# A four-block graph network on one core: TensorE's products in up to three parts, and another order for four engines

## The chip, the core and the metric

One core of a Trainium2 chip runs the whole network in one program. The metric is the device time of that core in microseconds, from a launch; the profile is of one further execution. Five queues work in parallel and meet only by semaphores: TensorE (PE in the profile, its weight loads PEld), VectorE (DVE), ScalarE (ACT), GpSimd (POOL) and SyncE (SP), which issues the DMAs.

## What is computed

x is 128 graphs of 64 nodes with 384 features, adj a 0/1 matrix per graph. Four blocks follow each other, each on the normalized input and added to x:

```python
h = relu(layernorm(x)); x = x + L0(h, adj)        # two layers
h = relu(layernorm(x)); x = x + L1(h, adj, adj)   # 12 heads
h = relu(layernorm(x)); x = x + L2(h, adj)        # 12 heads
h = relu(layernorm(x)); x = x + L3(h, adj)        # two layers
# L0, a layer: u = h (h Wl)^T above and on the diagonal, h (h Wr)^T below, / sqrt(384)
#   e = exp(u) * adj;  ctx = (e / sum e) @ (h W + b);  h = relu(layernorm(ctx) * a + b)
# L1, L2: softmax(q k^T / sqrt(384) + bias) @ v, then @ Wo + bo
# L3, a layer: att = softmax(h h^T / sqrt(384)) * adj, each row divided by its sum
#   ctx = upper(att) @ (h Wl^T + bl) + diag(att) * (h Ws^T + bs) + lower(att) @ (h Wr^T + br)
#   h = relu(layernorm(ctx) * g + b)
```

All in float32. Each product with a weight matrix is made of three reduced-precision ones: weights and tokens are split into a high and a low part, and high x high, low x high and high x low are summed in PSUM.

## The kernel before

The 8192 tokens are 32 groups of 256 (four graphs). Two streams, 0 and 1, each with its own SBUF and PSUM (four banks), take the groups in turn, 16 rounds per phase. There are four phases, one for each block: GCN0 (`gcn0_phase`, line 411), twice attention (`attention_phase`, from 821) and GCN3 (`gcn3_phase`, from 1228). The activations go through DRAM between phases.

What an engine does for one stream and one round is cut into named stages. Each engine's order of stages is written out by hand, as a string for each of TensorE, ScalarE, VectorE and GpSimd (in this sequence in each list): `GCN0_ORDERS`, `ATT_ORDERS`, `GCN3_ORDERS` for a round, `BETWEEN` for the seam from one phase to the next. A word like `hT_1.1'` is stage hT of layer 1 for stream 1, and the mark ' says that it belongs to the round before. An engine runs its string strictly in order; a stage waits for semaphores at its start or inside, and the values that it waits for are counted from the strings (`Count`, `counts`). The first two rounds are written out, the other 14 are a loop; `w0` to `w5` in `BETWEEN` are the splits of the next phase's weight matrices.

Stages that the prediction speaks of:

- TensorE: `ml0..2`, `mr0..2`, `lin0..1` (GCN0), `q`, `k0..2`, `v`, `out` (attention), `w00..w21` (GCN3) are products: 9 matmuls for each of 256 columns (ml, mr, q, k: weights stationary) or 384 columns (lin, v, out, w: tokens stationary), issued by `exact_product` (L226). The nine are in three groups of three: the first six use the high part of the tokens, the last three the low part. `q` holds three such products, `v` and `out` two. `hT` are six transpositions (L726, L1096, L1616), `aT` one, `u` and `scores` the node by node products, `agg` and `pv` the sums over neighbours, `pt0..2` four transpositions each of the softmax (L1177; pv is L1191, scores L1160).
- VectorE: `split` cuts hT into its high and low part (L1496, L1498), `agg` makes the statistics of a layer norm (in GCN0 L689 and L694), `ln` applies them (L706 in GCN0, L1592 in GCN3, two instructions of 128x384 each), `out` adds the residual (L628, L1482: scalar_tensor_tensor of 128x768 with both tensors in SBUF), `v` takes v from PSUM (L1028), `beta` is L620.
- GpSimd: `agg` is one pow on 128x2 between VectorE's agg and ln (L514, L1366); `p` scales two thirds of the softmax (L924, before pt1 and pt2); `w0`, `w1` add a bias (L1347); `z` and `diag` are other elementwise steps.
- ScalarE: `hT`, `q`, `k`, `pt0..2` (L982), `pv` copy PSUM to SBUF; `norm` is the input's layer norm.

`hT_1` starts the second layer and waits for VectorE's `ln_0` of its stream:

```python
pe.wait_ge(dve_done[s], DV[s]("n_0", i))          # GCN0 and GCN3, hT of layer 1
pe.wait_ge(pool_done[s], PO[s](f"p{c}", i))       # attention, pt1 and pt2
pe.wait_ge(act_done[s], AC[s].all(i, ("pt0", 0), ("pt1", 0), ("pt2", 0)))   # pv
```

## Time and profile before

| | us |
|---|---|
| median of 3 runs (2810.28 to 2812.11) | 2811.89 |
| span of the profiled execution | 2807.3 |
| TensorE busy, matmuls (98% of the span) | 2738.0 |
| VectorE busy (72%) | 2029.9 |
| GpSimd busy (51%) | 1434.8 |
| ScalarE busy (46%) | 1281.6 |

TensorE issues 34304 matmuls and as many weight loads. A busy share is an average over the span: that TensorE is busy for 98% says that it is the bound and that 69 us of its span are idle, not where. Matmuls overlap in the profile, so an idle stretch between two is counted only from the modelled end of the first. The timelines give start and length of an instruction, or of a run of equal ones (x4), and in brackets the idle time before it and what released it.

### The profile page before, as it was taken

Reading aid. Unit: us, or ns where it says so; the run is one execution under the profiler, and the core shown is the slowest. Engines: PE = TensorE matmul, PEld = TensorE weight load, DVE = VectorE, ACT = ScalarE, POOL = GpSimd, SP = SyncE. Lnnn points to the kernel's source line nnn. Section 1 sums busy time; section 2 is a strip of 40 time slices with the busy share of each in tenths; the row PEclk is TensorE's granted clock in tenths of the full one; section 3 lists DMA queues with packets and bytes.
Section 4 is the critical chain, followed back from the end, with each engine's and each line's share of the span. In section 5 each row is a group of like instructions: output and inputs, shape, how many; then the busy total and the mean of one; then the engine's idle time right before and its main releaser. Section 6 shows DMA issues by size and latency. Waiting matters only on the chain.

```text
span 2807.3 us, 86091 instructions
## 1 busy us (share of the span) xinstructions
PE 2738.0 (98%) x34304; PEld 2536.4 (90%) x34304; DVE 2029.9 (72%) x3998; ACT 1281.6 (46%) x2069; POOL 1434.8 (51%) x2499
## 2 busy tenths in 40 slices
PE   7999999999999999999989999999999999999998
PEld 7999999999988999999989999999888888888887
DVE  4666666766687777777777777778667767776776
ACT  3334334334344444444444444444545545445443
POOL 1212212122224555555545555555777777778777
PEclk9999999999999999999999999999999999999999
DMA  4121121211112111111131111112112112111121
GB/s 155 43 78 45 56 67 41 82 41 62 62 55 84 49 49 49 49 49 49 43 101 49 49 49 49 49 49 68 39 39 75 37 42 70 37 64 48 37 75 34
DMA packets 116535, 158.88 MB, mean 57 GB/s; under 512 B 8048, under 2 KB 112368, under 8 KB 116464
## 3 DMA queue, kind: packets, MB, share of 16 engines
q1 hardware_dynamic: 116464, 157.88, 17.2%
q8 instruction: 51, 0.84, 0.1%
q14 instruction: 20, 0.16, 0.0%
HBM read 107.52 MB, written 50.33 MB: 56 GB/s over the span
## 4 chain that ended last, share of the span: by engine, by line
PE 52%; POOL 25%; issue 12%; DVE 5%; ACT 3%; DMA 1%; POOLq 1%; SPq 0%; DVEq 0%; ACTq 0%
PE ps L226 38%; POOL wide L1347 6%; POOL wide L933 5%; POOL wide L924 4%; PE ps L1160 3%; PE ps L786 2%; PE ps L1191 2%; POOL wide L1332 2%; PE ps L809 2%; POOL wide L1336 2%; PE ps L1177 2%; PE ps L726 2%; ACT wide L996 2%; POOL rstd L1366 1%; POOL x_rstd L891 1%
## 5 line engine op out<-in xcount | busy, mean ns | idle before, releaser
L226 PE MATMUL ps<-w_hi,split 128*128 128x384 f32 x4608 | 1269.2, 344 | 8.3 <-ACT wide L962 4.6
L226 PEld LDWEIGHTS ps<-w_hi,split 128*128 128x128 f32 x4608 | 847.5, 190 | 23.8 <-ACT wide L962 5.0
L226 PE MATMUL ps<-split,w_hi 128*128 128x256 f32 x4608 | 865.0, 283 | 1.7 <-DVE split L640 1.6
L226 PE MATMUL ps<-w_lo,split 128*128 128x384 f32 x2304 | 778.3, 338 | 1.6 <-issue 1.6
L226 PEld LDWEIGHTS ps<-split,w_hi 128*128 128x128 f32 x4608 | 724.5, 189 | 25.3 <-issue 13.8
L226 PE MATMUL ps<-split,w_lo 128*128 128x256 f32 x2304 | 575.5, 280 | 0.0
L226 PEld LDWEIGHTS ps<-w_lo,split 128*128 128x128 f32 x2304 | 436.5, 189 | 0.0
L226 PEld LDWEIGHTS ps<-split,w_lo 128*128 128x128 f32 x2304 | 435.4, 189 | 0.0
L933 POOL TENSOR_TENSOR wide<-wide 128x192 f32<-128x192 f32 x256 | 212.3, 858 | 405.3 <-ACT wide L996 405.3
L1347 POOL TENSOR_TENSOR wide<-wide,row 128x192 f32<-128x192 f32 x512 | 312.6, 645 | 29.8 <-ACT wide L1430 29.8
L514 POOL TENSOR_TENSOR rstd<-mv,pos_half 128x2 f32<-128x2 f32 x64 | 43.6, 691 | 453.4 <-DVE mv L694 453.4
L1430 ACT ACTIVATE wide<-ps 128x768 f32<-128x768 f32 x128 | 103.2, 806 | 248.3 <-PE ps L226 248.1
L924 POOL TENSOR_TENSOR wide<-wide,heads 128x512 f32<-128x512 f32 x128 | 163.4, 1296 | 82.0 <-DVE heads L1064 82.0
L996 ACT ACTIVATE wide<-ps 128x768 f32<-128x768 f32 x64 | 52.0, 812 | 239.7 <-PE ps L226 239.7
L982 ACT ACTIVATE wide<-ps 128x512 f32<-128x512 f32 x192 | 110.6, 598 | 102.2 <-PE ps L1177 54.7
L1077 DVE TENSOR_TENSOR split<-ps,split 128x384 fp32r<-128x384 f32 x128 | 65.4, 553 | 126.6 <-ACT split L991 126.5
L916 POOL TENSOR_TENSOR wide<-xin,bo_row 128x192 f32<-128x192 f32 x256 | 147.6, 609 | 3.6 <-DMA x_after<-wide 3.6
L972 ACT ACTIVATE wide<-wide 128x1536 f32<-128x1536 f32 x64 | 95.2, 1487 | 98.3 <-DVE wide L1047 98.3
L947 ACT ACTIVATE wide<-xin,x_shift,x_rstd 128x384 f32<-128x384 f32 x128 | 83.7, 701 | 100.9 <-POOL x_shift L894 100.9
L1177 PE MATMUL ps<-ident,wide 128*128 128x128 f32 x768 | 118.0, 278 | 8.2 <-POOL wide L924 5.9
L1496 DVE CAST split<-wide 128x768 fp32r<-128x768 f32 x64 | 42.4, 662 | 111.3 <-ACT wide L1394 66.3
L1036 DVE TENSOR_TENSOR wide<-ps,bias 128x1536 f32<-128x1536 f32 x64 | 112.0, 1749 | 11.2 <-PE ps L1160 11.1
(131 smaller groups left out, 4549.6 us busy)
## 6 DMA issues: line engine op xcount, KB each, us to landing
x_after<-wide SPq DMA_DIRECT2D x96, 384.0 KB, 2.5
xin<-x_after SPq DMA_DIRECT2D x96, 384.0 KB, 3.4
xin<-in_x SPq DMA_DIRECT2D x32, 384.0 KB, 4.1
wide<-in_x SPq DMA_DIRECT2D x32, 384.0 KB, 3.6
wide<-x_after SPq DMA_DIRECT2D x32, 384.0 KB, 4.1
out<-wide SPq DMA_DIRECT2D x32, 384.0 KB, 2.8
adjin<-in_adj SPq DMA_DIRECT2D x32, 256.0 KB, 3.6
w_raw<-in_w SPq DMA_DIRECT2D x3, 2304.0 KB, 13.7
```

The costliest lines, as they stand in the source:

```text
L226: last = nc.tensor.matmul(out, t if tokens_stay else w, w if tokens_stay else t, start=(k == 0), stop=(k == len(pairs) - 1))
L916: ins = nc.gpsimd.tensor_tensor(b.xout[:, rows, at], b.xin[:, rows, at], bo_row[:, at], ALU.add)
L924: nc.gpsimd.tensor_tensor(b.e_rows[:, c * n:(c + 1) * n], b.e_rows[:, c * n:(c + 1) * n], b.factor[:, c * n:(c + 1) * n].unsqueeze(2).broa ...
L933: ins = nc.gpsimd.tensor_tensor(b.xout[:, rows, at], b.xout[:, rows, at], b.o_raw[:, rows, at], ALU.add)
L972: nc.scalar.activation(b.e[:], b.e[:], ACT.Exp, scale=SCALE).then_inc(act_done[s], 1)
L982: nc.scalar.activation(b.pT[:, HPC * c:HPC * c + HPC], b.ps[:, c % 2, :], ACT.Copy)\
L996: nc.scalar.activation(b.o_raw, b.ps[:, 2:4, 0:FEAT], ACT.Copy).then_inc(act_done[s], 1)
L1036: nc.vector.tensor_tensor(b.s[:].rearrange("p c r k -> p r c k"), b.ps[:, :, 0:C * P].rearrange("p r (c k) -> p r c k", c=C), b.bias[:].re ...
L1160: mm = nc.tensor.matmul(b.ps[t * NODES:(t + 1) * NODES, r, c * P + gr * NODES:c * P + (gr + 1) * NODES], b.q[r * HD:(r + 1) * HD, c, at:at ...
L1177: mm = nc.tensor.transpose(b.ps[:, c % 2, r * P:(r + 1) * P], b.e[:, c, r], g.ident[:])
L1347: ins = nc.gpsimd.tensor_tensor(b.hw[:, rows, m, at], b.hw[:, rows, m, at], w_row[l][m][:, at], ALU.add)
L1430: nc.scalar.activation(b.hw[:, :, m], b.ps_w[m], ACT.Copy).then_inc(act_done[s], 1)
```

## The change

Every product can be issued in parts. `exact_product` gets a first and a last group out of three (a, b, c); `parted` and `pieces` make a stage for every run of groups, so that `lin0ab_1.0'` is the first six matmuls of `lin0` and `lin0c_1.0'` the last three. A part that begins a product waits as the product did, the part that ends it signals. No matmul is added or removed, and a stage without letters is the whole product. In attention `q`, `v` and `out` become `q0..q2`, `v0..v1` and `out0..out1`, in the same sequence.

The strings are another order of the same stages. In the rounds of GCN0, among others, TensorE's `hT_1.0'` and `hT_1.1'` come ahead of the last third of a product and agg_0.1' ahead of two thirds of ml2; VectorE's out.0' moves from behind lin_0.1 to between agg_0.1 and ln_0.1. In attention's rounds only TensorE's order changes: a third of k2 stands between pt1 and pt2. In GCN3 w20a_0.1 goes ahead of hT_1.0, hT_1.1 ahead of w20c_1.0, hT_0.1 ahead of most of w01 and w10, and the orders of ScalarE, VectorE and GpSimd change too. In the seams `v.0` stands ahead of `beta.1'` on VectorE (GCN0 to attention), v.0 is issued in four parts around pt0.1', pt1.1', pt2.1' and hT.1 (attention to attention), and scores.1' comes ahead of pt0.0', u_0.0 ahead of pt0.1' and ScalarE's w2 and w3 ahead of its pt stages (attention to GCN3).

The diff, without the second and third seam and without the like edits of the other product stages:

```diff
 GCN0_ORDERS = [
-    "ml0_0.1' mr0_0.1' agg_0.0' ml1_0.1' ml2_0.1' mr1_0.1' mr2_0.1' lin0_0.1' hT_1.0' u_0.1' lin1_0.1' "
-    "ml0_1.0' ml1_1.0' aT_0.1' ml2_1.0' agg_0.1' mr0_1.0' mr1_1.0' mr2_1.0' lin0_1.0' hT_1.1' u_1.0' "
-    "lin1_1.0' mr0_1.1' ml0_1.1' mr1_1.1' mr2_1.1' aT_1.0' ml1_1.1' ml2_1.1' hT_0.0 agg_1.0' u_1.1' "
-    "ml0_0.0 mr0_0.0 lin0_1.1' mr1_0.0 mr2_0.0 ml1_0.0 ml2_0.0 lin1_1.1' aT_1.1' u_0.0 agg_1.1' hT_0.1 "
-    "lin0_0.0 aT_0.0 lin1_0.0",
-    "hT_1.1' soft_1.0' norm.0 aT_1.0' mr_1.1' ml_1.1' hT_0.0 z_1.0' soft_1.1' mr_0.0 norm.1 ml_0.0 "
-    "aT_1.1' soft_0.0 hT_0.1 z_1.1' aT_0.0 z_0.0 ml_0.1 mr_0.1 hT_1.0 soft_0.1 aT_0.1 z_0.1 ml_1.0 mr_1.0",
-    "split_1.1' soft_1.0' stat.0 att_1.0' sum_1.0' lin_1.0' split_0.0 agg_1.0' soft_1.1' ln_1.0' att_1.1' "
-    "stat.1 lin_1.1' sum_1.1' soft_0.0 att_0.0 gain.0' beta.0' split_0.1 lin_0.0 sum_0.0 agg_1.1' agg_0.0 "
-    "ln_0.0 split_1.0 soft_0.1 att_0.1 lin_0.1 out.0' sum_0.1 ln_1.1' agg_0.1 ln_0.1 gain.1' beta.1' "
-    "out.1'",
-    "agg_0.1' stat.0 agg_1.0' stat.1 adj_1.1 adj_0.0 adj_0.1 agg_0.0 agg_1.1' adj_1.0",
+    "ml0_0.1' mr0_0.1' ml1a_0.1' agg_0.0' ml1bc_0.1' ml2_0.1' mr1_0.1' mr2_0.1' lin0ab_0.1' hT_1.0' "
+    "lin0c_0.1' u_0.1' lin1_0.1' ml0_1.0' ml1ab_1.0' aT_0.1' ml1c_1.0' ml2a_1.0' agg_0.1' ml2bc_1.0' "
+    "mr0_1.0' mr1_1.0' mr2_1.0' lin0ab_1.0' hT_1.1' lin0c_1.0' u_1.0' lin1ab_1.0' mr0a_1.1' "
+    "lin1c_1.0' mr0bc_1.1' ml0_1.1' mr1_1.1' mr2_1.1' ml1ab_1.1' aT_1.0' ml1c_1.1' ml2_1.1' hT_0.0 "
+    "agg_1.0' u_1.1' lin0a_1.1' ml0_0.0 mr0_0.0 mr1_0.0 mr2_0.0 lin0b_1.1' ml1_0.0 ml2ab_0.0 "
+    "lin0c_1.1' ml2c_0.0 lin1_1.1' aT_1.1' u_0.0 agg_1.1' hT_0.1 lin0_0.0 aT_0.0 lin1_0.0",
+    "hT_1.1' soft_1.0' norm.0 aT_1.0' mr_1.1' ml_1.1' hT_0.0 z_1.0' soft_1.1' mr_0.0 ml_0.0 norm.1 "
+    "aT_1.1' soft_0.0 hT_0.1 z_1.1' aT_0.0 z_0.0 ml_0.1 mr_0.1 hT_1.0 soft_0.1 aT_0.1 z_0.1 ml_1.0 "
+    "mr_1.0",
+    "split_1.1' soft_1.0' stat.0 att_1.0' sum_1.0' lin_1.0' split_0.0 soft_1.1' agg_1.0' ln_1.0' "
+    "att_1.1' stat.1 lin_1.1' soft_0.0 sum_1.1' att_0.0 gain.0' split_0.1 beta.0' lin_0.0 sum_0.0 "
+    "agg_1.1' agg_0.0 ln_0.0 split_1.0 soft_0.1 att_0.1 lin_0.1 sum_0.1 ln_1.1' agg_0.1 out.0' "
+    "ln_0.1 gain.1' beta.1' out.1'",
+    "agg_0.1' stat.0 agg_1.0' stat.1 adj_1.1 adj_0.0 adj_0.1 agg_1.1' agg_0.0 adj_1.0",
 ]
 ATT_ORDERS = [
-    "q.1' k0.1' k1.1' v.1' pt0.0' hT.0 pt1.0' pt2.0' k2.1' pv.0' scores.1' out.0' q.0 k0.0 k1.0 v.0 "
-    "pt0.1' hT.1 pt1.1' pt2.1' k2.0 pv.1' scores.0 out.1'",
-    "q.1' norm.0 pt0.0' hT.0 pt1.0' pt2.0' k.1' pv.0' out.0' exp.1' q.0 norm.1 pt0.1' hT.1 pt1.1' pt2.1' "
-    "k.0 pv.1' out.1' exp.0",
-    "stat.0 abs.0' fac.0' v.1' hT.0 pv.0' s.1' soft.1' stat.1 abs.1' fac.1' v.0 hT.1 pv.1' s.0 soft.0",
+    "q0.1' q1.1' q2.1' k0.1' k1.1' v0.1' v1.1' pt0.0' hT.0 pt1.0' k2a.1' pt2.0' k2bc.1' pv.0' "
+    "scores.1' out0.0' out1.0' q0.0 q1.0 q2.0 k0.0 k1.0 v0.0 v1.0 pt0.1' hT.1 pt1.1' k2a.0 pt2.1' "
+    "k2bc.0 pv.1' scores.0 out0.1' out1.1'",
+    "q.1' norm.0 pt0.0' hT.0 pt1.0' pt2.0' k.1' pv.0' out.0' exp.1' q.0 norm.1 pt0.1' hT.1 pt1.1' "
+    "pt2.1' k.0 pv.1' out.1' exp.0",
+    "stat.0 abs.0' fac.0' v.1' hT.0 pv.0' s.1' soft.1' stat.1 abs.1' fac.1' v.0 hT.1 pv.1' s.0 "
+    "soft.0",
     "bias.1' stat.0 bias.0 p.0' xb.1' out.0' stat.1 p.1' xb.0 out.1'",
 ]
 GCN3_ORDERS = [
-    "hT_0.0 agg_1.0' u_0.0 aT_1.1' w20_1.1' w21_1.1' w00_0.0 w01_0.0 w10_0.0 hT_0.1 w11_0.0 u_0.1 "
-    "agg_1.1' aT_0.0 w20_0.0 w21_0.0 w00_0.1 agg_0.0 aT_0.1 w01_0.1 w10_0.1 w11_0.1 hT_1.0 w20_0.1 "
-    "w21_0.1 w00_1.0 w01_1.0 agg_0.1 u_1.0 w10_1.0 w11_1.0 w20_1.0 hT_1.1 w21_1.0 u_1.1 aT_1.0 w00_1.1 "
-    "w01_1.1 w10_1.1 w11_1.1",
-    "soft_0.1' swap_0.1' on_0.0' tiny_0.1' w0_0.1' w1_0.1' hT_1.0' on_0.1' w0_1.0' swap_1.0' w1_1.0' "
+    "hT_0.0 agg_1.0' u_0.0 aT_1.1' w20_1.1' w21_1.1' w00_0.0 w01a_0.0 hT_0.1 w01bc_0.0 w10_0.0 "
+    "w11_0.0 u_0.1 agg_1.1' aT_0.0 w20_0.0 w21_0.0 w00_0.1 agg_0.0 aT_0.1 w01_0.1 w10_0.1 w11_0.1 "
+    "w20a_0.1 hT_1.0 w20bc_0.1 w21_0.1 w00_1.0 w01_1.0 agg_0.1 u_1.0 w10_1.0 w11_1.0 w20ab_1.0 "
+    "hT_1.1 w20c_1.0 w21_1.0 u_1.1 aT_1.0 w00_1.1 w01_1.1 w10_1.1 w11_1.1",
+    "soft_0.1' on_0.0' swap_0.1' tiny_0.1' w0_0.1' w1_0.1' hT_1.0' on_0.1' w0_1.0' swap_1.0' w1_1.0' "
     "tiny_1.0' soft_1.0' hT_1.1' soft_1.1' tiny_1.1' swap_1.1' w0_1.1' norm.0 hT_0.0 on_1.0' w1_1.1' "
     "soft_0.0 swap_0.0 norm.1 w0_0.0 hT_0.1 on_1.1' w1_0.0 tiny_0.0",
-    "sum_1.0' diag_1.0' split_1.1' soft_1.1' stat.0 w2_1.0' att_1.1' sum_1.1' stat.1 aT_1.0' split_0.0 "
-    "diag_1.1' aT_1.1' soft_0.0 agg_1.0' w2_1.1' att_0.0 ln_1.0' split_0.1 soft_0.1 sum_0.0 diag_0.0 "
-    "aT_0.0 agg_1.1' w2_0.0 att_0.1 sum_0.1 agg_0.0 diag_0.1 ln_0.0 split_1.0 aT_0.1 w2_0.1 ln_1.1' "
-    "agg_0.1 out.0' ln_0.1 soft_1.0 out.1' att_1.0",
-    "agg_0.1' on_1.0' diag_1.0' adj_0.0 w0_1.0' stat.0 on_1.1' w1_1.0' stat.1 adj_1.0 w0_1.1' w1_1.1' "
-    "adj_0.1 diag_1.1' agg_1.0' adj_1.1 w0_0.0 on_0.0 w1_0.0 diag_0.0 z.0' on_0.1 agg_1.1' agg_0.0 "
-    "diag_0.1 w0_0.1 w1_0.1 z.1'",
+    "sum_1.0' diag_1.0' split_1.1' soft_1.1' stat.0 att_1.1' sum_1.1' stat.1 w2_1.0' aT_1.0' "
+    "diag_1.1' split_0.0 soft_0.0 agg_1.0' aT_1.1' att_0.0 w2_1.1' split_0.1 ln_1.0' soft_0.1 "
+    "sum_0.0 diag_0.0 agg_1.1' att_0.1 aT_0.0 w2_0.0 sum_0.1 agg_0.0 ln_0.0 diag_0.1 aT_0.1 "
+    "split_1.0 w2_0.1 ln_1.1' agg_0.1 out.0' ln_0.1 soft_1.0 out.1' att_1.0",
+    "agg_0.1' on_1.0' diag_1.0' adj_0.0 w0_1.0' stat.0 w1_1.0' on_1.1' adj_1.0 stat.1 w0_1.1' "
+    "w1_1.1' agg_1.0' adj_0.1 diag_1.1' adj_1.1 w0_0.0 on_0.0 w1_0.0 diag_0.0 on_0.1 z.0' agg_0.0 "
+    "agg_1.1' diag_0.1 w0_0.1 w1_0.1 z.1'",
 ]
 BETWEEN = [
     [
-        "ml0_0.1' agg_0.0' mr0_0.1' ml1_0.1' ml2_0.1' mr1_0.1' mr2_0.1' hT_1.0' lin0_0.1' u_0.1' lin1_0.1' "
-        "aT_0.1' ml0_1.0' agg_0.1' ml1_1.0' ml2_1.0' mr0_1.0' mr1_1.0' mr2_1.0' hT_1.1' lin0_1.0' u_1.0' "
-        "mr0_1.1' ml0_1.1' lin1_1.0' aT_1.0' mr1_1.1' mr2_1.1' ml1_1.1' ml2_1.1' agg_1.0' u_1.1' lin0_1.1' "
-        "lin1_1.1' aT_1.1' hT.0 agg_1.1' q.0 hT.1 k0.0 k1.0 v.0 k2.0 scores.0",
-        "hT_1.1' w0 w1 w2 soft_1.0' aT_1.0' norm.0 mr_1.1' ml_1.1' z_1.0' soft_1.1' aT_1.1' hT.0 z_1.1' "
-        "norm.1 w3 hT.1 q.0 k.0 exp.0",
-        "split_1.1' soft_1.0' stat.0 att_1.0' w0 sum_1.0' lin_1.0' stat.1 w1 w2 agg_1.0' soft_1.1' att_1.1' "
-        "ln_1.0' lin_1.1' sum_1.1' hT.0 gain.0' beta.0' out.0' agg_1.1' hT.1 ln_1.1' gain.1' w3 beta.1' v.0 "
-        "out.1' s.0 soft.0",
+        "ml0_0.1' mr0a_0.1' agg_0.0' mr0bc_0.1' ml1_0.1' ml2_0.1' mr1_0.1' mr2_0.1' hT_1.0' "
+        "lin0_0.1' u_0.1' lin1_0.1' ml0ab_1.0' aT_0.1' ml0c_1.0' ml1a_1.0' agg_0.1' ml1bc_1.0' "
+        "ml2_1.0' mr0_1.0' mr1_1.0' mr2_1.0' lin0a_1.0' hT_1.1' lin0bc_1.0' u_1.0' lin1a_1.0' "
+        "mr0_1.1' ml0_1.1' mr1a_1.1' lin1bc_1.0' mr1bc_1.1' aT_1.0' mr2_1.1' ml1_1.1' ml2_1.1' "
+        "agg_1.0' u_1.1' hT.0 lin0_1.1' lin1_1.1' q0a.0 aT_1.1' q0b.0 agg_1.1' q0c.0 q1.0 q2.0 "
+        "k0ab.0 hT.1 k0c.0 k1.0 v0.0 v1.0 k2.0 scores.0",
+        "hT_1.1' soft_1.0' w0 w1 w2 aT_1.0' norm.0 mr_1.1' ml_1.1' z_1.0' hT.0 soft_1.1' aT_1.1' w3 "
+        "z_1.1' norm.1 q.0 hT.1 k.0 exp.0",
+        "split_1.1' soft_1.0' stat.0 att_1.0' sum_1.0' stat.1 lin_1.0' w0 w1 w2 agg_1.0' soft_1.1' "
+        "ln_1.0' att_1.1' lin_1.1' hT.0 sum_1.1' gain.0' w3 beta.0' agg_1.1' hT.1 ln_1.1' out.0' "
+        "gain.1' v.0 beta.1' out.1' s.0 soft.0",
         "agg_0.1' stat.0 stat.1 bias.0 agg_1.0' agg_1.1' xb.0",
     ],
...
@@ -214,18 +223,42 @@
     return not isinstance(i, int) or i > 0
 
 
-def exact_product(nc, out, terms, tokens_stay=False, tokens_lo_made=None):
+PARTS = "abc"
+
+
+def parted(stages):
+
+    return {piece: (whole, first, last) for whole in stages for first in range(len(PARTS))
+            for last in range(first, len(PARTS))
+            for piece in {whole + PARTS[first:last + 1]} | ({whole} if last - first == len(PARTS) - 1 else set())}
+
+
+def ends(events):
+
+    return {piece: names for whole, names in events.items() for piece, (_, _, last) in parted([whole]).items()
+            if last == len(PARTS) - 1}
+
+
+def pieces(stages):
+
+    def cut(stage, first, last):
+        return lambda s, i: stage(s, i, first, last)
+    return {piece: cut(stages[whole], first, last) for piece, (whole, first, last) in parted(stages).items()}
+
+
+def exact_product(nc, out, terms, first, last, tokens_stay=False, tokens_lo_made=None):
 
 
 
     pairs = [(w, t_hi) for w_hi, w_lo, t_hi, _ in terms for w in (w_hi, w_lo)]
     pairs += [(w_hi, t_lo) for w_hi, _, _, t_lo in terms]
-    for k, (w, t) in enumerate(pairs):
+    for k in range(len(terms) * first, len(terms) * (last + 1)):
+        w, t = pairs[k]
         if k == 2 * len(terms) and tokens_lo_made is not None:
             tokens_lo_made()
-        last = nc.tensor.matmul(out, t if tokens_stay else w, w if tokens_stay else t,
-                                start=(k == 0), stop=(k == len(pairs) - 1))
-    return last
+        mm = nc.tensor.matmul(out, t if tokens_stay else w, w if tokens_stay else t,
+                              start=(k == 0), stop=(k == len(pairs) - 1))
+    return mm
 
 
 class Shared:
...
             def ml(o):
-                def stage(s, i):
-                    if o == 0:
+                def stage(s, i, first, last):
+                    if o == 0 and first == 0:
                         weights_made(pe, g, phase, 3 * l + LEFT, i)
                         pe.wait_ge(dve_done[s], DV[s](f"t_hi_{l}", i))
-                    mm = project_T(s, i, bufs[s].rows[l], LEFT, o)
-                    if o == C - 1:
+                    mm = project_T(s, i, bufs[s].rows[l], LEFT, o, first, last)
+                    if o == C - 1 and last == len(PARTS) - 1:
                         mm.then_inc(pe_done[s], 1)
                 return stage
 
...
-        def q(s, i):
-            def tokens_lo_made():
-                pe.wait_ge(dve_done[s], DV[s]("t_lo", i))
-            pe.wait_ge(act_done[s], AC[s]("t_hi", i))
-            o_taken(s, i, 0)
-            weights_made(pe, g, phase, WQ, i)
-            project_T(bufs[s], bufs[s].ps_row, WQ, chunks=(0, 1), tokens_lo_made=tokens_lo_made)
-            o_taken(s, i, 1)
-            project_T(bufs[s], bufs[s].ps_row, WQ, chunks=(2,)).then_inc(pe_done[s], 1)
-
-        def k(c):
-            def stage(s, i):
-                if c == 0:
+        def q(o):
+            def stage(s, i, first, last):
+                def tokens_lo_made():
+                    pe.wait_ge(dve_done[s], DV[s]("t_lo", i))
+                if first == 0:
+                    if o == 0:
+                        pe.wait_ge(act_done[s], AC[s]("t_hi", i))
+                        o_taken(s, i, 0)
+                        weights_made(pe, g, phase, WQ, i)
+                    if o == C - 1:
+                        o_taken(s, i, 1)
+                mm = project_T(bufs[s], bufs[s].ps_row, WQ, o, first, last, tokens_lo_made=tokens_lo_made)
+                if o == C - 1 and last == len(PARTS) - 1:
+                    mm.then_inc(pe_done[s], 1)
+            return stage
+
...
```

## Rows read from the trace of the kernel before

**Rows 1.** stretches: length, then busy us of PE, PEld, DVE, ACT, POOL, clock, DMA

```profile
40.00:790.00 750.00, 749.68 (x8174) 687.98 (x8172) 497.89 (x1317) 293.45 (x545) 159.29 (x360) 1.00 0.18 60
790.00:912.00 122.00, 111.61 (x1664) 105.72 (x1663) 99.96 (x153) 54.24 (x82) 48.95 (x72) 0.97 0.26 80
912.00:1370.00 458.00, 454.41 (x7835) 438.73 (x7835) 359.94 (x448) 220.92 (x316) 259.75 (x395) 1.00 0.15 48
1975.00:2760.00 785.00, 778.48 (x6166) 689.41 (x6166) 554.00 (x1393) 393.85 (x673) 598.63 (x1088) 1.00 0.15 50
```

**Rows 2.** who TensorE waited for: idle us in total, times, longest

```profile
PE ps L1616 <- DVE wide L1592: 7.0, 15, 0.5
PE ps L1177 <- POOL wide L924: 5.9, 26, 0.2
PE ps L226 <- ACT wide L962: 4.6, 2, 2.3
PE ps L1160 <- DVE wide L1028: 2.1, 1, 2.1
```

**Rows 3.** timeline of a GCN0 round: start us, us, engine, line; TensorE, VectorE, GpSimd

```profile
450.79 0.69 PE L226 MATMUL ps<-w_hi,split 128*128 128x384 f32 x3
451.32 0.82 PE L726 MATMUL ps<-ident,wide 128*128 128x128 f32 x6
...
448.90 0.15 DVE L694 BATCH_NORM_AGGREGATE mv<-st 128x2 f32<-128x6 f32 x1
450.26 0.87 DVE L706 TENSOR_SCALAR wide<-wide,mv,rstd 128x384 f32<-128x384 f32 x2
...
449.13 0.69 POOL L514 TENSOR_TENSOR rstd<-mv,pos_half 128x2 f32<-128x2 f32 x1 [10.62 <-DVE mv L694]
```

**Rows 4.** timeline of a GCN3 round about hT_1.0; VectorE, GpSimd, TensorE

```profile
2351.40 1.56 DVE L1592 TENSOR_SCALAR wide<-wide,mv,rstd 128x384 f32<-128x384 f32 x2 [0.62 <-POOL rstd L1366]
...
2351.48 2.49 POOL L1347 TENSOR_TENSOR wide<-wide,row 128x192 f32<-128x192 f32 x4
...
2353.02 0.87 PE L1616 MATMUL ps<-ident,wide 128*128 128x128 f32 x6 [0.48 <-DVE wide L1592]
```

**Rows 5.** the same round about hT_1.1; VectorE, GpSimd, TensorE

```profile
2364.49 0.96 DVE L1482 SCALAR_TENSOR_TENSOR wide<-wide 128x768 f32<-128x768 f32 x1
...
2366.04 0.87 DVE L1592 TENSOR_SCALAR wide<-wide,mv,rstd 128x384 f32<-128x384 f32 x2 [0.60 <-POOL rstd L1366]
...
2364.54 1.47 POOL L1366 TENSOR_TENSOR rstd<-rstd,neg_half 128x2 f32<-128x2 f32 x1 [0.52 <-DVE rstd L1567]
...
2367.19 0.82 PE L1616 MATMUL ps<-ident,wide 128*128 128x128 f32 x6
```

**Rows 6.** timeline of attention about pt2 and pv, rounds and seam; TensorE, ScalarE

```profile
1200.72 0.65 PE L1177 MATMUL ps<-ident,wide 128*128 128x128 f32 x4 [0.23 <-POOL wide L924]
1201.13 0.36 PE L226 MATMUL ps<-split,w_hi 128*128 128x256 f32 x1
...
1202.36 0.45 PE L1191 MATMUL ps<-wide 64*32 64x64 f32 x31
...
1200.80 1.21 ACT L982 ACTIVATE wide<-ps 128x512 f32<-128x512 f32 x2
...
1219.77 0.34 PE L1191 MATMUL ps<-wide 64*32 64x64 f32 x16
...
1218.37 1.08 ACT L982 ACTIVATE wide<-ps 128x512 f32<-128x512 f32 x2
...
1396.79 0.60 ACT L982 ACTIVATE wide<-ps 128x512 f32<-128x512 f32 x1 [0.32 <-PE ps L1177]
...
1397.53 0.69 PE L1191 MATMUL ps<-wide 64*32 64x64 f32 x48
```

**Rows 7.** timeline of VectorE ahead of v.0 in the first seam

```profile
827.52 1.20 DVE L620 TENSOR_TENSOR wide<-wide,row 128x768 f32<-128x768 f32 x1
828.65 0.94 DVE L1028 TENSOR_TENSOR wide<-ps,bv_row 128x768 f32<-128x768 f32 x1
```

172 lines of the change are left out of this document (97 added, 75 removed), and 31 rows, old and new, of the table BETWEEN.

## The prediction

> **What bounds the kernel now.** I read the windows by phase first: what each engine does there, and how much of the stretch TensorE is idle [rows 1]. In the rounds of the first phase TensorE is idle for 0.3 us of 750; in the first attention phase's rounds for 3.6 of 458; in the last phase's for 6.5 of 785; the seam into attention loses 10 of 122, with the granted clock at 0.97. VectorE is busy for two thirds to four fifths, so only TensorE is a bound by its work. What a reordering can win is therefore what TensorE waits for. The list of its waits says for whom [rows 2]: hT_1 of the last phase for the layer norm on VectorE (L1592, 15 times), pt2 of attention for GpSimd's scaling (L924, 26 times), and the seams. The rest comes from short timelines of one steady round per phase. The idle column starts at the modelled end of the last matmul, and a transposition that waits for nothing starts 0.16 us before that end: the row of three products at 450.79 ends at 451.48, hT_1.1 starts at 451.32 [rows 3]. So a wait of 0.48 in the list costs 0.64. The same two rows give the length of a third of a product with 384 columns: 0.53 us.
>
> **Last phase, hT_1.0.** Its input is ready at 2352.96 (L1592 starts at 2351.40 and takes 1.56) and it starts at 2353.02, 0.06 later, with 0.48 of idle before it [rows 4]. The change puts w20a_0.1 in front: 0.53 of 0.64 are covered. The two L1592 take 0.87 together elsewhere [rows 5], and 1.56 here because GpSimd's L1347 runs beside them from 2351.48 [rows 4]. The new GpSimd order puts the small agg_1.1' (a pow on 128x2, 0.69 in [rows 3]) ahead of diag_0.1 and w0_0.1, so that L1347 begins some 0.7 later and the norm should be ready earlier than TensorE gets there: I take the whole wait as gone, 15 x 0.64 = -9.6. Bounds: -15 x 0.53 if the norm stays at 1.56, and the loss of the third rival. What is late next is the split behind hT_1.0, because w00_1.0 follows 0.53 sooner: 0 to 0.2 a round, I take 0.07, +1.0.
>
> **Last phase, hT_1.1.** It moves ahead of w20c_1.0, 0.53 earlier. Its input (L1592 from 2366.04 for 0.87) is ready at 2366.91, and it started at 2367.19 [rows 5]. It would now be issued at 2366.66 and wait until 2366.97: 0.31. Queued behind it are w20c, w21 and u_1.1; the last then has 0.5 more cover for its own input, so I take 0.25: 15 x 0.25 = +3.8. Why its input is late stands in the same rows: out.0' (L1482, both inputs in SBUF, 0.96) starts at 2364.49 on VectorE, the pow L1366 starts 0.05 later on GpSimd and takes 1.47 in place of 0.69.
>
> **First phase, hT_1.1.** Before, VectorE ran out.0' ahead of sum_0.1, and agg_0.1 was followed by ln_0.1 at once: statistics end at 449.05, the pow takes 0.69 from 449.13, ln_0.1's large pair (L706) ends at 451.13, hT_1.1 starts at 451.32 [rows 3]. The new VectorE order is agg_0.1 out.0' ln_0.1, the pair that costs 1.47 in the last phase, with the same form of instruction (L628 as L1482, 128x768 from SBUF) and the same start order. The new TensorE order issues agg_0.1 six 256-column products earlier (six of the nine in 1.23 us [rows 6], 0.7 to 0.8; I take 0.70), so the statistics end at 448.35 and the pow starts 0.08 later, at 448.43, as before. With 1.47 [rows 5] it ends at 449.90; L706 starts 0.44 after a pow's end and takes 0.87 [rows 3]: 451.21, and 0.06 to TensorE: 451.27. TensorE gets there at 451.32 - 0.53 = 450.79. Wait 0.48, of which I take 0.47; nothing else of TensorE may pass it, and its rounds had no slack. Without out.0' behind it (round 0) and in the seam, where more products stand between, it doesn't appear: 14 x 0.47 = +6.6. Bounds 0 (pow at 0.69) and +6.6. The other thirds in this phase fill no wait, since there was none; I cost them at 0, hidden by the products that follow.
>
> The Trainium skill (SBUF — State Buffer, Who interferes with whom) says that a VectorE instruction with two SBUF inputs contends with a GpSimd instruction that reads SBUF. The 1.47 against 0.69 agrees, and it speaks against this change. The same section says that the loser blocks for the whole instruction; the 1.56 of L1592 beside three L1347 is less than that would give, and the rows decide.
>
> **Attention.** In round 10, stream 0, pt2 waits for GpSimd until 1200.72: 0.23 of idle, 0.39 with the overlap. k2a (a third of the nine products between 1201.13 and 1202.36, 0.41) now stands before it and covers that. But pv is next, 0.41 sooner, and it needs ScalarE's two L982 that end at 1202.01 [rows 6]. How soon pv follows such a copy shows in the seam: copy ended at 1397.39, pv at 1397.53, 0.14 [rows 6]. So pv starts at 1202.01 + 0.03 + 0.14 = 1202.18 where it started at 1202.36: 0.18 of 0.39 is won, and the rest becomes a wait for ScalarE. In stream 1 the copies end at 1219.45 and pv starts at 1219.77; the products now push pt2 and its copy back by 0.15, and nothing is won. Net 0.17 a round, 28 rounds of the two phases: -4.7. Bounds: 0, and -28 x 0.6 if the copies weren't in the way. q, v and out in single parts have the same instructions: 0. ScalarE's, VectorE's and GpSimd's orders of these rounds don't change.
>
> **Seams and start.** Into attention scores.0 waits 2.1 for v.0 on VectorE [rows 2]. v.0 (from 828.65) stood behind beta.1' (1.20, [rows 7]) and moves ahead of it, but s.0, which heads the chain to the next 2.3 us wait, then stands behind beta.1' and out.1': of 1.2 I keep 1.0. Between the attention phases the parts of v.0 now stand ahead of pt1.1 and pv.1, which waited for copies there (0.32 of idle before the one, 0.12 before the other, each with its 0.16 of overlap [rows 6]): -0.6, the rest of it in the bounds. Into the last phase u_0.0 loses pt0.1' as its cover, four transpositions, 0.41 as those from 1200.72 to 1201.13 [rows 6]: +0.4; w2 and w3 on ScalarE ahead of the pt copies are hidden behind out.0', which waits for VectorE's pv.0' (L1077) in any case; at the start ml1a covers 0.3 of agg_0.0's wait. Together -1.5, bounds -5 and +2. The waits with no releaser and the stretches at the lower clock stay.
>
> **The sum.** -9.6 + 1.0 + 3.8 + 6.6 - 4.7 - 1.5 = -4.4 us. The profiled span is 2807.3, the median of the runs 2811.9: I apply the difference to the median, 2807.5, -0.16%.
>
> **Rivals.** (1) out.0' and the pow don't meet as in the last phase (the pow takes 0.69): no wait at hT_1.1 in either phase, -4.4 - 6.6 - 3.8 = -14.8, 2797.1. For it: in the first phase the order before never had the two together. Against: same form, same order, and the 1.47 is in the rows. 0.20. (2) The thirds only move waits: attention gives 0 (pv takes all of it), the seams 0: 2813.7. For it: 0.35 and 0.32 between copy and pv is all the room there is. 0.20. (3) Slower: the pow of agg_1.1', now just ahead of ln_0.0, holds VectorE instead of L1347 doing so. The norm then ends 0.69 later, at 2353.65, hT_1.0 waits 2353.71 - 2352.91 = 0.80 instead of 0.64, and -9.6 becomes +2.4: +7.6, 2819.5. It decides from a wait of 0.70 at hT_1.0. By the rule of the section named above this is what should happen if the pow issues first. Against: pow and norm read little of what the other holds, and the norm beside nothing but a pow isn't in the rows. 0.15. My own case 0.40; 0.05 for what I don't see.
>
> **Numbers.** About 0.2% (5.6 us) is what a measurement of this kernel can tell from no change. My case spans 2802 to 2812 and lies on both sides of that bound: nearly half of it counts as faster. Faster 0.18 + 0.20 = 0.38, within 0.2% 0.44, slower 0.18. The range takes in rival 1 and most of the way to rival 3: 2797 to 2818.
>
> **What would show it.** In the list of waits: L1616 for L1592 down in total but some 0.15 each at hT_1.1; a new line L726 for L706, 14 times 0.3; L1177 for L924 nearly gone; L1191 for L982 up to about 30 entries. GpSimd's L514 at 1.47 fourteen times. I am wrong if L514 stays at 0.69 throughout, if L1592 is at or above 0.7 at ln_0.0, or if the rounds of any phase hold a wait on an operation not named here, such as w2_1.1' ahead of hT_0.1, which moves 15 products forward.

## The result, and the profile after

The changed kernel takes 2825.5 us (median of 4 runs, 2823.6 to 2828.0) where the kernel before, timed beside it, takes 2811.1 (2809.5 to 2812.1): a ratio of 1.0051, 95% interval 1.0038 to 1.0064. The forecast was 2807.5 with a range of 2797 to 2818. The time is 14.4 us above the kernel before and outside the range, and even the rival that ended slower, 2819.5, fell short of it.

The span of the profiled execution is 2824.4 us. The totals hardly differ from before, and the list of what TensorE waited for is the first thing to read (columns: idle us in total, times, longest; rows of the start and the seams left out at the dots):

```profile
PE 2746.0 (97%) x34304; PEld 2535.7 (90%) x34304; DVE 2032.7 (72%) x3998; ACT 1283.9 (45%) x2069; POOL 1461.1 (52%) x2499
...
PE ps L1660 <- DVE small L1586: 7.4, 14, 1.8
...
PE ps L760 <- DVE wide L740: 5.6, 25, 0.2
...
PE ps L1743 <- DVE wide L1551: 3.4, 14, 1.1
...
PE ps L1219 <- POOL wide L959: 0.9, 2, 0.7
```

Lines have moved by 33 to 48: L760 is hT of the first phase, L740 its `ln`; L1660 is hT of the last phase, L1586 the copy of aT, L1551 `w2`, L1743 `agg`; L1219 is pt, L959 GpSimd's scaling. The two large rows of [rows 2] are gone as forecast (L1592, 15 times; L924 from 26 times to 2). In their place stand three rows that the forecast has only in part: hT_0.0 for aT's copy, hT_1 of the first phase 25 times and not 14, and `agg` for `w2`.

The windows say in which phase it happens (stretches as in [rows 1]):

```profile
40.00:790.00 750.00, 744.22 (x8038) 673.39 (x8037) 494.49 (x1295) 288.22 (x536) 162.82 (x355) 1.00 0.18 59
790.00:912.00 122.00, 114.26 (x1556) 107.94 (x1556) 98.70 (x168) 54.37 (x81) 47.00 (x73) 0.97 0.24 76
912.00:1370.00 458.00, 454.79 (x8026) 442.60 (x8024) 362.07 (x447) 222.82 (x319) 258.93 (x395) 1.00 0.15 49
1975.00:2760.00 785.00, 772.95 (x6150) 679.27 (x6150) 543.99 (x1365) 390.36 (x666) 608.57 (x1068) 1.00 0.15 50
```

TensorE's idle time grew from 0.3 to 5.8 us in the first phase's stretch and from 6.5 to 12.1 in the last's. The clock is the same, stretch by stretch.

The sharpest measure is the length of a round: from the start of stream 0's input transposition (hT_0.0, in attention hT.0) in round 4 to that in round 14, a tenth of it. It agrees within 0.15 us between kernels with the same orders, and 14 times the sum of the differences (attention twice, for its two phases) gives each total below within 3.5 us, e12 (5) and e7 (10) apart. For the change: 14 x (0.98 + 0.79) - 28 x 0.38 = 14.1, of 14.4 measured.

| kernel | median us | ratio to before, 95% | GCN0 | attention | GCN3 |
|---|---|---|---|---|---|
| before | 2811.1 | | 49.63 | 34.96 | 51.48 |
| changed | 2825.5 | 1.0038 to 1.0064 | 50.61 | 34.58 | 52.27 |
| e1_stat1_behind | 2812.6 | 1.0001 to 1.0019 | 50.58 | 34.59 | 51.40 |
| e2_pow_first | 2818.1 | 1.0021 to 1.0050 | 50.04 | 34.60 | 52.33 |
| e3_out_back | 2817.5 | 1.0018 to 1.0038 | 50.16 | 34.59 | 52.40 |
| e4_tensor_rounds | 2798.0 | 0.9955 to 0.9979 | 49.80 | 34.59 | 51.37 |
| e5_others_rounds | 2830.9 | 1.0067 to 1.0097 | 50.39 | 34.95 | 52.57 |
| e6_seams_only | 2806.9 | 0.9980 to 0.9998 | 49.70 | 34.95 | 51.49 |
| e7_fixes | 2827.0 | 1.0042 to 1.0072 | 49.66 | 34.59 | 52.76 |
| e8_diag_behind | 2798.4 | 0.9941 to 0.9967 | 49.70 | 34.95 | 50.83 |
| e9_best | 2793.5 | 0.9918 to 0.9945 | 49.70 | 34.60 | 50.95 |
| e10_three_back | 2799.8 | 0.9947 to 0.9974 | 49.80 | 34.59 | 51.39 |
| e11_two_thirds | 2809.9 | 0.9991 to 1.0009 | 49.67 | 35.19 | 50.83 |
| e12_out1_early | 2830.3 | 1.0050 to 1.0077 | 50.64 | 34.59 | 52.37 |
| e13_diag_and_thirds | 2798.3 | 0.9940 to 0.9974 | 49.69 | 34.60 | 51.41 |
| e14_best_seams | 2788.2 | 0.9912 to 0.9947 | 49.67 | 34.59 | 50.84 |

The kernel before, run beside them, had medians of 2808.8 (e1 to e8), 2809.6 (e9 to e12) and 2810.2 us (e13, e14).

**Where the last phase lost it.** One steady round about hT_0.0 (VectorE, then SyncE's DMAs, then TensorE):

```profile
2378.24 0.95 DVE L1526 SCALAR_TENSOR_TENSOR wide<-wide 128x768 f32<-128x768 f32 x1
...
2386.23 1.02 DVE L1511 BATCH_NORM_STATS2 x_st<-xin 128x6 f32<-128x384 f32 x2 [1.08 <-DMA xin<-x_after]
...
2387.45 0.92 DVE L1551 TENSOR_TENSOR wide<-ps,row 128x768 f32<-128x768 f32 x1
2388.30 0.41 DVE L1586 TENSOR_TENSOR small<-ps,parts 128x256 f32<-128x256 f32 x1
...
2379.38 0.40 SPq L367 DMA_DIRECT2D out<-wide  x1
...
2381.43 0.37 SPq L356 DMA_DIRECT2D xin<-x_after  x1
...
2388.76 0.87 PE L1660 MATMUL ps<-ident,wide 128*128 128x128 f32 x6 [0.59 <-DVE small L1586]
```

out.1' (L1526) ends at 2379.19. Only then can SyncE store it (2379.38), and the load of x for the next round is issued behind the store (2381.43). stat.1 (L1511) reads that x and starts 7.04 us after out.1' has ended, having stood idle for 1.08. The change put w2_1.0' (L1551, 0.92) behind stat.1 and ahead of aT_1.0' (L1586), for which hT_0.0 waits. The kernel before had the same load, with stat.1 (L1467 there) 6.9 us behind out.1', but w2_1.0' (L1507) ran while it was under way, VectorE stood for 0.1 only, and aT_1.0' (L1542) followed stat.1 at once:

```profile
2373.22 0.93 DVE L1507 TENSOR_TENSOR wide<-ps,row 128x768 f32<-128x768 f32 x1
...
2375.18 1.02 DVE L1467 BATCH_NORM_STATS2 x_st<-xin 128x6 f32<-128x384 f32 x2
...
2376.40 0.39 DVE L1542 TENSOR_TENSOR small<-ps,parts 128x256 f32<-128x256 f32 x1
```

The 0.92 has moved from beside the load to behind it.

**Where the first phase lost it.** One round about both hT_1 (VectorE, GpSimd, TensorE):

```profile
441.75 0.41 DVE L734 TENSOR_SCALAR rstd<-rstd 128x2 f32<-128x2 f32 x1 [0.80 <-POOL rstd L548]
...
442.40 1.18 DVE L740 TENSOR_SCALAR wide<-wide,mv,rstd 128x384 f32<-128x384 f32 x2
...
453.82 0.96 DVE L662 SCALAR_TENSOR_TENSOR wide<-wide 128x768 f32<-128x768 f32 x1
...
455.77 0.87 DVE L740 TENSOR_SCALAR wide<-wide,mv,rstd 128x384 f32<-128x384 f32 x2
...
441.68 0.46 POOL L534 TENSOR_TENSOR small<-adjin,ones 128x128 f32<-128x128 f32 x1
442.10 0.88 POOL L539 TENSOR_TENSOR small<-adjin,tri 128x128 f32<-128x128 f32 x2
453.95 1.38 POOL L548 TENSOR_TENSOR rstd<-mv,pos_half 128x2 f32<-128x2 f32 x1 [10.96 <-DVE mv L728]
...
443.64 0.87 PE L760 MATMUL ps<-ident,wide 128*128 128x128 f32 x6 [0.23 <-DVE wide L740]
...
456.69 0.88 PE L760 MATMUL ps<-ident,wide 128*128 128x128 f32 x6 [0.22 <-DVE wide L740]
```

The second half is the forecast: the pow beside out.0' (L662) takes 1.38, and hT_1.1 waits. The first half isn't in it: adj_1.0 (L534, L539) now follows the pow of agg_0.0 at once and runs beside ln_0.0. It costs twice there. The small L734 at the head of ln_0.0, which starts 0.07 behind L534, takes 0.41 where it takes 0.17 in ln_0.1 and in the kernel before, and the two L740 take 1.18 where they took 1.02 before (0.87 in ln_0.1). Together that is 0.4, and hT_1.0 waits as well.

### The profile page after: what moved, and what is told of

The parts are those of the page before. It is cut to its first block, busy times and chain, and to the rows that moved or that the text cites. A ratio compares the mean times of both kernels' runs of the same rounds, so it can differ in the third digit from the quotient of the medians.

```text
span 2824.4 us, 86091 instructions
## 1 busy us (share of the span) xinstructions
PE 2746.0 (97%) x34304; PEld 2535.7 (90%) x34304; DVE 2032.7 (72%) x3998; ACT 1283.9 (45%) x2069; POOL 1461.1 (52%) x2499
## 4 chain that ended last, share of the span: by engine, by line
PE 65%; issue 12%; POOL 11%; DVE 7%; DMA 3%; ACT 1%; SPq 1%; POOLq 0%; DVEq 0%; ACTq 0%
PE ps L259 48%; POOL wide L1391 4%; PE ps L1219 3%; PE ps L1202 3%; PE ps L1233 3%; PE ps L820 2%; PE ps L843 1%; PE ps L1743 1%; DMA xin<-x_after 1%; PE ps L1131 1%; PE ps L760 1%; POOL wide L1376 1%; POOL wide L1380 1%; POOL rstd L1410 1%; DMA adjin<-in_adj 1%
## 5 line engine op out<-in xcount | busy, mean ns | idle before, releaser
L259 PE MATMUL ps<-split,w_lo 128*128 128x256 f32 x2304 | 589.8, 284 | 0.0
L1391 POOL TENSOR_TENSOR wide<-wide,row 128x192 f32<-128x192 f32 x512 | 343.2, 705 | 39.4 <-ACT wide L1474 39.4
L548 POOL TENSOR_TENSOR rstd<-mv,pos_half 128x2 f32<-128x2 f32 x64 | 54.5, 851 | 460.4 <-DVE mv L728 460.4
L959 POOL TENSOR_TENSOR wide<-wide,heads 128x512 f32<-128x512 f32 x128 | 165.0, 1308 | 81.7 <-DVE heads L1099 81.7
L982 ACT ACTIVATE wide<-xin,x_shift,x_rstd 128x384 f32<-128x384 f32 x128 | 83.7, 701 | 98.6 <-POOL x_shift L929 98.5
L1071 DVE TENSOR_TENSOR wide<-ps,bias 128x1536 f32<-128x1536 f32 x64 | 112.0, 1749 | 12.3 <-PE ps L1202 12.1
L1219 PE MATMUL ps<-ident,wide 128*128 128x128 f32 x768 | 117.8, 276 | 1.4 <-POOL wide L959 0.9
```

The lines of the kernel that those rows point to most:

```text
L259: mm = nc.tensor.matmul(out, t if tokens_stay else w, w if tokens_stay else t, start=(k == 0), stop=(k == len(pairs) - 1))
L959: nc.gpsimd.tensor_tensor(b.e_rows[:, c * n:(c + 1) * n], b.e_rows[:, c * n:(c + 1) * n], b.factor[:, c * n:(c + 1) * n].unsqueeze(2).broa ...
L1071: nc.vector.tensor_tensor(b.s[:].rearrange("p c r k -> p r c k"), b.ps[:, :, 0:C * P].rearrange("p r (c k) -> p r c k", c=C), b.bias[:].re ...
L1219: mm = nc.tensor.transpose(b.ps[:, c % 2, r * P:(r + 1) * P], b.e[:, c, r], g.ident[:])
L1391: ins = nc.gpsimd.tensor_tensor(b.hw[:, rows, m, at], b.hw[:, rows, m, at], w_row[l][m][:, at], ALU.add)
```

## The experiments

The theory after the result: the new orders of VectorE and GpSimd lose what TensorE's new order gains, at three single stages. The rival: TensorE's own order makes the waits, by taking transpositions out from behind the products that covered their inputs.

**e1_stat1_behind.** The changed kernel, last phase, VectorE:

```diff
-... sum_1.1' stat.1 w2_1.0' aT_1.0' diag_1.1' ...
+... sum_1.1' w2_1.0' aT_1.0' stat.1 diag_1.1' ...
```

> The changed kernel with one stage moved in the last phase's VectorE order: stat.1 behind aT_1.0' instead of ahead of w2_1.0'. Theory: the 0.59 us a round that hT_0.0 waits there for aT_1.0' (7.4 us in 14 waits in the list) is VectorE standing before stat.1, 1.08 us in the round shown, for a load of x that lands later, with w2_1.0' and aT_1.0' queued behind it. Then hT_0.0's wait is gone: 14 x 0.59 = 8.3 less, 2825.5 - 8.3 = 2817, 1.002 of the kernel before. Rival: aT_1.0' is late because VectorE as a whole is late at this place (it is busy from out.1' on), and stat.1 merely takes its turn elsewhere: then hT_0.0 keeps 0.5 or more a round, or the same wait turns up at a later stage, and the time stays within 2 us of 2825.5.

2812.6 us, and 0.87 off the round. VectorE no longer stops at the load, and hT_0.0 follows its products at once:

```profile
2374.95 0.96 DVE L1551 TENSOR_TENSOR wide<-ps,row 128x768 f32<-128x768 f32 x1
2375.83 0.41 DVE L1586 TENSOR_TENSOR small<-ps,parts 128x256 f32<-128x256 f32 x1
2376.20 1.02 DVE L1511 BATCH_NORM_STATS2 x_st<-xin 128x6 f32<-128x384 f32 x2
...
2377.96 0.82 PE L1660 MATMUL ps<-ident,wide 128*128 128x128 f32 x6
```

The theory holds; its size, 0.59 a round, was too small. Over the rounds measured hT_0.0 had lost 0.61 (0.45 of idle and the 0.16 of overlap that the forecast had added in its own terms), and hT_0.1's wait for w2_1.1' (L1660 <- L1551, 0.21) went too.

**e2_pow_first and e3_out_back.** The changed kernel, first phase, one stage each (GpSimd; VectorE):

```diff
-... agg_1.1' agg_0.0 adj_1.0
+... agg_0.0 agg_1.1' adj_1.0
```

```diff
-... lin_0.1 sum_0.1 ln_1.1' agg_0.1 out.0' ln_0.1 ...
+... lin_0.1 out.0' sum_0.1 ln_1.1' agg_0.1 ln_0.1 ...
```

> The changed kernel with two small stages of the first phase's GpSimd order swapped back: the pow agg_0.0 ahead of the pow agg_1.1'. Theory: in the change the pow of agg_0.0 is the second of the two, so that GpSimd's adj_1.0 (1.30 us) starts right at ln_0.0, whose two instructions then take 1.83 us together in place of 1.27, and hT_1.0 waits 0.36 us a round. With the swap undone ln_0.0 has only a small pow beside it at its start: L740 there about 1.3 to 1.5, hT_1.0 waits 0 to 0.1: 14 x 0.3 = 4 to 5 less, 2821. Rival: the wait comes from hT_1.0 being issued a third of a product (0.53 us) sooner, whatever GpSimd does: L740 stays at 1.8 or the wait stays at 0.3, and the time at 2825.

> The changed kernel with one stage moved back in the first phase's VectorE order: out.0' ahead of sum_0.1, as in the kernel before, so that ln_0.1 follows agg_0.1 at once. Theory (the fourth term of the prediction): the pow L548 of agg_0.1, 1.38 us beside out.0', takes 0.69 again, and hT_1.1 loses its wait of 0.39 us a round: 14 x 0.39 = 5.5 less, 2820. Rival: out.0' in its old place delays agg_0.1 itself (it started 0.77 us after VectorE had come free, and out.0' takes 0.96), so at most 0.5 of 0.69 is won, or another stage comes late; then hT_1.1 keeps 0.2 or more and the time is at 2823 or above.

Both theories hold: 0.57 and 0.45 off the round. hT_1.0 had waited 0.38 and hT_1.1 0.38; the rest of e2's 0.57 is no wait, 0.15 of it is spread over matmuls that follow each other some 5 ns sooner late in the round. e2 first, then e3 (VectorE, GpSimd, TensorE in each):

```profile
388.75 1.02 DVE L740 TENSOR_SCALAR wide<-wide,mv,rstd 128x384 f32<-128x384 f32 x2
...
387.62 1.34 POOL L548 TENSOR_TENSOR rstd<-mv,pos_half 128x2 f32<-128x2 f32 x2 [10.18 <-DVE mv L728]
388.93 0.62 POOL L534 TENSOR_TENSOR small<-adjin,ones 128x128 f32<-128x128 f32 x1
...
389.84 0.86 PE L760 MATMUL ps<-ident,wide 128*128 128x128 f32 x6
```

```profile
401.33 0.87 DVE L740 TENSOR_SCALAR wide<-wide,mv,rstd 128x384 f32<-128x384 f32 x2
...
400.20 0.69 POOL L548 TENSOR_TENSOR rstd<-mv,pos_half 128x2 f32<-128x2 f32 x1 [11.00 <-DVE mv L728]
...
402.52 0.82 PE L760 MATMUL ps<-ident,wide 128*128 128x128 f32 x6
```

In e2 a second small pow stands between ln_0.0 and adj_1.0 (the x2 of 1.34), L740 is back at the 1.02 of the kernel before, and hT_1.0 starts without a wait. In e3 the pow is back at 0.69, and hT_1.1 starts without one.

**e4_tensor_rounds and e5_others_rounds.** Only TensorE's round orders are new; only the other three engines' are. Seams as before in both.

> The changed kernel's order of TensorE in the rounds of all three kinds of phase, with the kernel before's orders for VectorE, ScalarE and GpSimd in the rounds and for all four engines in the seams. Theory: the loss of the change comes from the other three engines' new orders, and TensorE's own new order gains. Attention keeps its whole gain, since the other orders hardly differ there (34.96 to 34.59 us a round, 28 x 0.38 = 10.5 less); the last phase's rounds lose the wait for aT_1.0' and most of the 0.64 at hT_1.0 (51.48 to about 51.2, 4 less); the first phase's rounds stay at 49.63 (within 0.2). Together about 2811 - 14 = 2797, ratio 0.995. Rival: TensorE's order itself makes the new waits, by taking hT_1.0, hT_1.1 and hT_0.1 ahead of products that covered their inputs: then the first phase's rounds go to 50.2 or more and the last phase's to 51.8 or more, and the time is 2811 or above.

> The mirror of the kernel with TensorE's new rounds alone: TensorE's rounds of the kernel before, the changed kernel's orders for ScalarE, VectorE and GpSimd in the rounds, all seams as before. Theory: the other three engines' orders carry the loss by themselves. The last phase keeps the wait of hT_0.0 for aT_1.0' (0.5 to 0.6 us a round) and loses the 0.64 at hT_1.0, since ln_0.0 is ready earlier: 51.4 to 51.7 us a round. In the first phase hT_1.0 is hidden (it is issued 0.53 later than in the change), hT_1.1 waits 0.5 to 0.7 for the pow beside out.0': 50.1 to 50.3. Attention stays at 34.96. Sum 14 x 0.55 + 14 x 0.1 = 9 more than before: 2818. Rival: the new orders were fitted to each other, and without TensorE's every stage of theirs meets the wrong neighbour: a wait on an operation that neither kernel has, the last phase's rounds at 52.2 or more and the time at 2830.

e4 landed where the theory put it: 2798.0. TensorE's new order is not the loss. Attention keeps its whole gain; the first phase loses 0.17 a round, with no wait in it that the kernel before hadn't. In the last phase only 0.11 is gained: its waits are now hT_1.0 (0.14), hT_1.1 (0.29) and the split behind hT_1.0 (0.13). e5 shows the loss without TensorE, and there the rival did better: 2830.9 is its number and not the theory's 2818. The first phase came near to what was expected (50.39, L760 for L740 14 times), the last at 52.57, above the theory's 51.4 to 51.7. One row carries that, which the changed kernel has at a quarter of the size:

```profile
PE ps L1743 <- DVE wide L1551: 13.6, 16, 1.1
PE ps L1660 <- DVE small L1586: 9.9, 14, 1.5
```

agg_0.0 waits for w2_0.0, which the new VectorE order puts behind att_0.1 as well.

**e6_seams_only.** The three seams of the change in the kernel before.

> The kernel before with the changed kernel's three seams alone, all four engines. The prediction's term: -1.5 us, bounds -5 and +2, so 2807.3 with the rounds at 49.63, 34.96 and 51.48 as before. Rival: the seams lose what the whole change shows beyond its rounds, which is 14.4 - 14 x 0.96 + 28 x 0.38 - 14 x 0.77 = 0.8 more: 2809.6. A third case: more than 3 us either way would say that the seams hold a cost that the sum over the rounds hides.

2806.9 beside 2808.8. The interval, 0.6 to 5.6 us less, holds the forecast's -1.5.

**e7_fixes.**

```diff
-... agg_0.0 diag_0.1 ln_0.0 split_1.0 aT_0.1 w2_0.1 ln_1.1' agg_0.1 out.0' ln_0.1 soft_1.0 ...
+... agg_0.0 ln_0.0 diag_0.1 split_1.0 aT_0.1 w2_0.1 ln_1.1' agg_0.1 ln_0.1 out.0' soft_1.0 ...
```

> A version put together from what the runs so far say: the first phase and all seams as in the kernel before, attention's and the last phase's TensorE rounds from the change, the other engines' orders as before but for two stages of the last phase's VectorE: diag_0.1 behind ln_0.0, so that GpSimd's bias adds (L1391) begin only after the norm, and out.0' behind ln_0.1, so that the pow of agg_0.1 (L1410) has no instruction with two SBUF inputs beside it. Theory: against TensorE's new rounds alone (2798.0) the first phase gives back 14 x 0.17 = 2.4, hT_1.0 14 x 0.14 = 2.0 and hT_1.1 14 x 0.19 = 2.6: 2791, ratio 0.9937; L1636 at ln_0.0 takes 0.9 for the two and L1410 0.69. Rival: with the norm faster the next in line waits (the split behind hT_1.0, or load of x behind the later out.0'), and the last phase's rounds stay above 51.2: 2795 or more.

A plain miss: 52.76 us a round in the last phase, the worst of all kernels. The pow takes 0.70, as it should, but out.0' comes later, its store and stream 0's load of x behind it, and VectorE stops before stat.0:

```profile
2380.59 1.02 DVE L1511 BATCH_NORM_STATS2 x_st<-xin 128x6 f32<-128x384 f32 x2 [1.83 <-DMA xin<-x_after]
...
2371.38 0.70 POOL L1410 TENSOR_TENSOR rstd<-rstd,neg_half 128x2 f32<-128x2 f32 x1
```

TensorE's row L1660 <- L1586 rose to 23.6 us in 14 waits. It is the loss of the change over again, made from the other end of the same chain, and for a wait at hT_1.1 of 0.29 (the 0.19 of the expectation was read too low).

**e8_diag_behind.** Of e7 the first of the two moves alone, in the kernel before, TensorE untouched.

> The kernel before with one stage moved: diag_0.1 behind ln_0.0 in the last phase's VectorE order, TensorE untouched. Theory: the 0.64 us a round that hT_1.0 lost comes from GpSimd's bias adds, let go by diag_0.1 just ahead of the norm (L1347 of the kernel before starts 0.08 after L1592, which then takes 1.56 for the two in place of 0.87); with diag_0.1 behind the norm that is 0.87 and the whole wait is gone without any third of a product: 15 x 0.64 = 9.6 less, 2799, last phase 50.85 us a round. Rival: the prediction's reason, the order of the two pows on GpSimd, is what counts, and diag_0.1 does nothing: 1.5 for the norm, 51.48 a round, 2809. Between them: diag_0.1 later makes diag_0.1's readers late on TensorE (agg_0.1), and half of it comes back as a wait there.

2798.4 beside 2808.8: the theory's number, with one stage moved. The norm ahead of hT_1.0, with GpSimd's bias adds behind it (VectorE, GpSimd, TensorE; before stands in [rows 4]):

```profile
2348.17 0.87 DVE L1636 TENSOR_SCALAR wide<-wide,mv,rstd 128x384 f32<-128x384 f32 x2 [0.80 <-POOL rstd L1410]
2348.96 0.28 DVE L1581 TENSOR_REDUCE diag<-small 128x2 f32<-128x128 f32 x1
...
2349.46 5.57 POOL L1391 TENSOR_TENSOR wide<-wide,row 128x192 f32<-128x192 f32 x8
...
2349.15 0.82 PE L1660 MATMUL ps<-ident,wide 128*128 128x128 f32 x6
```

In e4, with diag_0.1 ahead of the norm as before and only TensorE's order new, the same pair takes 1.57:

```profile
2338.91 1.57 DVE L1636 TENSOR_SCALAR wide<-wide,mv,rstd 128x384 f32<-128x384 f32 x2 [0.62 <-POOL rstd L1410]
...
2338.99 5.06 POOL L1391 TENSOR_TENSOR wide<-wide,row 128x192 f32<-128x192 f32 x8
```

**e9_best.** e8's stage and TensorE's new attention rounds.

> The kernel before with the two pieces that gained: diag_0.1 behind ln_0.0 in the last phase's VectorE order, and the changed kernel's TensorE order in attention's rounds. They lie in different phases, so their gains should add: 2798.4 - 28 x 0.37 = 2788, rounds of 49.65, 34.59, 34.59 and 50.84 us, ratio 0.992. Rival: the seams are written for the old rounds and give some of it back, 2793 or more.

2793.5, ratio 0.9918 to 0.9945. The rounds are as expected, the time is 5.5 us above it, on the rival's number. In the profile the seam between the attention phases is 5 us longer than in e8's, the one into attention 3 us shorter. Beyond whole rounds the former takes 18 to 24 us in the kernels with TensorE's new attention rounds and 16 to 19 in those with the old. The ranges touch (e4, with the new rounds, has 18.5), so that a part of the gain is given back there is likely and not shown.

**e10_three_back.** The stages of e1, e2 and e3 together.

> The changed kernel with all three single moves at once: stat.1 behind aT_1.0' (last phase, VectorE), agg_0.0 ahead of agg_1.1' (first phase, GpSimd), out.0' ahead of sum_0.1 (first phase, VectorE). Theory: the two waits of the first phase are independent, 50.59 - 0.54 - 0.43 = 49.62 us a round, the last phase 51.40 as with stat.1 alone: 2812.6 - 14 x 0.97 = 2799, ratio 0.996. Rival: in the first phase the first wait hides part of the second, so that the two together give less than their sum: 49.9 or more, 2803.

2799.8, as expected, by way of 49.80 us in the first phase and not 49.62. Both waits went in full (0.8 together); what is missing is the part of e2's gain that was no wait. 49.80 is also what e4 has. The changed kernel stands 14.4 us above the kernel before, with these three stages moved 9.9 below it: they cost it 24.

**e11_two_thirds.** e9 with `k2ab pt2 k2c` where it has `k2a pt2 k2bc`, both streams.

> The version put together of the two gains, with two thirds of k2 ahead of pt2 in attention instead of one, in both streams. Theory: with one third pt2 starts within 0.13 and 0.18 us of GpSimd's scaling, and pv then comes 1.43 us after pt2 starts (pt2 0.65, ScalarE's copy 0.60, 0.14 and 0.04 between), with TensorE idle before it; a further third moves pt2, its copy and pv back by its 0.35: 34.59 + 2 x 0.35 = 35.3 us a round, worse than the kernel before, 28 x 0.7 = 20 more than with one third. Rival: TensorE's work is the same and the second third only fills idle time: 34.6 or less.

35.19 against an expected 35.3, and 16 us more than e9 where 20 were expected: the second third costs most of what it weighs, 0.30 of 0.35 for each stream. Behind pt2 everything is a fixed chain through ScalarE, here from 1204.23 to 1205.61 with TensorE idle at its end:

```profile
1204.23 0.60 PE L1219 MATMUL ps<-ident,wide 128*128 128x128 f32 x4
...
1205.61 1.16 PE L1233 MATMUL ps<-wide 64*32 64x64 f32 x96 [0.42 <-ACT wide L1017]
...
1204.86 0.60 ACT L1017 ACTIVATE wide<-ps 128x512 f32<-128x512 f32 x1 [0.28 <-PE ps L1219]
```

**e12_out1_early.** The changed kernel with out.1' ahead of soft_1.0, stat.1 left in its bad place.

> The changed kernel with out.1' ahead of soft_1.0 in the last phase's VectorE order, stat.1 where the change puts it. Theory: SyncE stores what out.1' made and then loads x of the next round behind it; from the end of out.1' to the start of stat.1 were 7.05 us (2379.18 to 2386.23). With out.1' 0.53 earlier the load lands 0.53 earlier, stat.1, w2_1.0' and aT_1.0' follow, and the wait of hT_0.0 falls from 0.59 to about 0.1: 52.25 - 0.5 = 51.75 us a round, 14 x 0.5 = 7 less, 2818.5. Rival: it is another condition that lets the load go (the norm of the round before, or the bandwidth of the DMAs): stat.1 starts where it did relative to ln_0.1, and the round stays at 52.2.

The time went to 2830.3 and not to 2818.5. The wait before stat.1 did fall, from 1.08 to 0.26 in the round looked at, and hT_0.0's row to the second of these two:

```profile
PE ps L1721 <- ACT wide L1446: 6.4, 15, 0.4
PE ps L1660 <- DVE small L1586: 2.3, 5, 0.8
```

But the x did not come sooner. Counted from the end of ln_0.1, in the mean of rounds 4 to 14, out.1' ends 0.5 earlier and SyncE issues the load 0.4 earlier, and then the load takes 5.3 us to land where it took 4.7, so stat.1 starts 8.5 us behind ln_0.1 and not 8.3. That is the sign that the expectation gave to its rival: stat.1 stays where it was relative to ln_0.1. The wait is shorter because VectorE arrives later: soft_1.0, 0.95 later, holds ScalarE's soft and its copy of hT_1.1 behind it, and u_1.1 (L1721) waits 15 times. 52.37 a round, nothing won.

**e13_diag_and_thirds.** e9 with TensorE's new order in the last phase too.

> The best version so far (diag_0.1 behind ln_0.0, attention's new TensorE rounds) with the changed kernel's TensorE order in the last phase's rounds too. Theory: the thirds there have no wait left to fill at hT_1.0, and bring forward hT_1.1, whose norm stands behind the blocked pow, and w00_1.0: waits of about 0.19 and 0.13 us a round, last phase 50.94 + 0.3 = 51.2 us, 4 us more than the best version. Rival: the thirds still cover something, since the last phase's round has 0.4 us of waits left: 50.9 or less.

2798.3, last phase 51.41 and not 51.2: once the norm is fast, TensorE's thirds there cost 0.46 us a round (the largest waits: 0.29 at hT_1.1, 0.18 at the split behind hT_1.0). This equals e4's 51.37, where the norm was slow: with the thirds in place the fast norm is worth nothing, without them 0.65 a round.

**e14_best_seams.** e9 with the change's seams.

> The best version with all three seams of the change. The seams alone measured 1.9 us less than the kernel before (2806.9 against 2808.8), so 2791.6 against 2793.5, rounds of 49.70, 34.60, 34.60, 50.94 unchanged. Rival: the first rounds of a phase differ between kernels by several us without an order to blame, and the time lands anywhere within 5 us of 2793.

2788.2 us, ratio 0.9912 to 0.9947, the fastest kernel here. It is 5.3 us below e9 where 1.9 was expected, but the two intervals overlap, and that the seams are worth more than e6 showed isn't shown.

## Why the prediction was wrong, point by point

The step that failed is a price of nothing: the sum took its terms from the list of waits of before, and put every moved stage that has no row there at 0 or left it out. Those stages cost 22 us.

- **Last phase, hT_1.0, -9.6.** The wait went, as forecast: hT_1.0 follows its matmuls at once. The forecast's reason was that the pow of agg_1.1' now stands ahead of diag_0.1, so that the bias adds start 0.7 later. It stood ahead of it before as well, but ahead of agg_0.0 too; the change puts it between agg_0.0, which lets the norm go, and diag_0.1. In the kernel before nothing stood between:

```profile
2350.68 0.69 POOL L1366 TENSOR_TENSOR rstd<-rstd,neg_half 128x2 f32<-128x2 f32 x1 [2.55 <-DVE rstd L1567]
2351.33 0.20 POOL L1361 TENSOR_TENSOR diag<-diag,rasum 128x2 f32<-128x2 f32 x1
```

  An estimate from these rows and [rows 4]: with a second pow between them L1347 would start at 2352.17, and the norm, at 0.87, would end at 2352.27, so this might have been nearly enough. No run has it alone. What the forecast didn't price is VectorE's diag_0.1, moved behind ln_0.0, for which GpSimd's diag_0.1 waits. That is enough by itself (e8), and in the changed kernel it comes last (L1405; the two pows end at 2415.73):

```profile
2415.11 0.87 DVE L1636 TENSOR_SCALAR wide<-wide,mv,rstd 128x384 f32<-128x384 f32 x2 [0.82 <-POOL rstd L1410]
...
2414.37 1.36 POOL L1410 TENSOR_TENSOR rstd<-rstd,neg_half 128x2 f32<-128x2 f32 x2 [0.81 <-DVE rstd L1611]
2416.25 0.20 POOL L1405 TENSOR_TENSOR diag<-diag,rasum 128x2 f32<-128x2 f32 x1 [0.52 <-DVE diag L1581]
```

  This also settles the third rival: the norm takes 0.87 beside the pow, so the pow doesn't hold it. TensorE's third, to which the forecast gave 0.53 of the 0.64, wasn't needed (e8), and the thirds of the last phase together cost more than they gave (e13).
- **w00_1.0 behind it, +1.0.** The wait came, at 0.18 a round where 0.07 was taken: +2.5, inside the bound of 0.2.
- **Last phase, hT_1.1, +3.8.** Right: 0.24 a round for 0.25, with the pow at 1.47 beside out.0'.
- **First phase, hT_1.1, +6.6.** Right in mechanism and nearly in size: the pow took 1.38 for the 1.47 assumed, the wait was 0.38 for 0.47, and e3 got 0.45 a round back by taking out.0' away.
- **Attention, -4.7.** Right that pt2's wait goes and that pv's wait for ScalarE takes its place (pv starts 0.14 behind the copy in both streams), but half the size: 0.38 a round, not 0.17. Stream 0 gave the 0.2 forecast; the failed step is stream 1, costed at nothing because pt2's copy would come 0.15 later. pt2 came 0.14 later and its copy 0.05, since ScalarE was busy with the copy ahead of it and not waiting for pt2. [rows 6] had this: the two L982 of that stream take 1.08 together, those of stream 0 1.21.
- **Seams, -1.5.** Not contradicted (e6, -1.9).
- **What the sum left out.** Edits costed at nothing. In the first phase the swap of two pows on GpSimd brought adj_1.0 beside ln_0.0: 0.38 a round at hT_1.0 (e2: 0.57). TensorE's other thirds there, which the forecast put at 0, cost 0.17 (e4). In the last phase w2_1.0' went between stat.1 and aT_1.0': 0.61 (e1: 0.87 with what followed). And two `w2` stages came late, w2_1.1' ahead of hT_0.1 and w2_0.0 ahead of agg_0.0: 0.2 each. The forecast had named the first of these two as what would prove it wrong, and given it no price (what moves there is 15 matmuls, not 15 products). Together 1.6 us a round, 22 in 14 rounds. Attention gave 6 more than forecast, the other waits came out within 1.5 of their terms, and the miss is 18: some 2 us of it are in no term.
- **The range.** It was built around the waits that the list of before shows. A reordering can make a wait at each stage that it moves, and the list of before has no row for those. Their bounds were not zero.

The rule that the forecast quoted from the Trainium skill (SBUF — State Buffer, Who interferes with whom), that an instruction with two SBUF inputs on VectorE contends with a GpSimd instruction that reads SBUF, carried the two terms that came true. The forecast also read the 1.56 of the norm as less than its "fully blocks" would give. That doesn't follow: the 1.56 are two instructions, and one by one they look like taking turns. In e4 the two L1636 take 0.90 and 0.76, each 0.48 alone (e8), and the L1391 beside them 0.60, 0.72 and 0.71, each 0.60 in e8. Nor do they show that the loser waits for the whole of the other instruction: the norm beside the pow loses nothing (0.87).

On the store that holds back a load, the Trainium skill (DMA: Bandwidth & Descriptors, Anatomy of one DMA — SWDGE (gpsimd) path) says that semaphore waits happen on the issuing sequencer and not in the DMA engines. These DMAs are issued by SyncE; its rows agree, 0.19 us from the end of out.1' to its store and the load behind it in the same queue.

**Still open.** Kernels with the same orders in the first phase, the first seam and attention differ there by up to 8 us (e7 and e9), 5 of the 8 in waits of 1 to 3 us that the list puts down to "issue", in the first three rounds of the attention phase. That is as large as most of the 10 us by which e7's median lies above what its rounds give. No run here tells what they wait for.

## What to carry to other kernels

An engine that runs a fixed order stops at the slowest input of each stage, so an instruction that waits for a DMA must be placed by when the load lands, and what others wait for must stand ahead of it. Issuing the load sooner need not land it sooner (e12). In a reordering, price every stage that moves, on every engine, for what it now delays and for what it now runs beside; the largest win from one move here was a small VectorE stage (0.28 us) put behind a norm, because in its old place it let another engine's work collide with that norm. Where all waits are tenths of a microsecond, measure round by round and stage by stage: three moves made 2825 into 2800, and the best parts of both kernels give 2788 (before: 2810).

## What the runs showed of the hardware

- A pow on 128x2 on GpSimd takes 0.69 us, and 1.38 to 1.47 when it starts 0.05 to 0.13 us behind a scalar_tensor_tensor of VectorE with both inputs in SBUF (0.95). The mean of a line tells how often: L548 has 851 ns over 64 in the changed kernel and 690 in e3, 0.16 x 64 / 0.69 = 15 blocked ones.
- VectorE's tensor_scalar from SBUF loses to GpSimd's tensor_tensor, small ones too. On 128x384 one takes 0.48 us alone, 0.80 or 0.62 beside adj_1.0 (changed kernel, e2), 0.90 and 0.76 beside the bias adds of 128x192 (e4), which lose 0.1 each in turn. On 128x2 (L734) it takes 0.17, and 0.41 when it starts 0.07 behind a tensor_tensor of 128x128 on GpSimd (changed kernel). Beside a pow on 128x2 it loses nothing.
- From the end of out.1' to the start of stat.1 are 6.8 us in the kernel before and 6.9 in the changed one (means of rounds 4 to 14): 2.2 until SyncE has issued the store and three more DMAs down to the load of x, and 4.6 to 4.7 for its 384 KB to land. How long that takes goes with how close the other stream's load is ahead: 4.6 to 4.7 us where the two are issued 3.0 to 3.1 us apart (before, changed, e1, e4, e8, e10), 5.3 where they are 2.7 apart (e7, e12). The core's DMAs move up to 400 GB/s in that stretch.
